# Gated cross-attention with a mixture-of-experts layer: expert rows turned by VectorE instead of TensorE

## The reference

```python
x = x + tanh(g_xattn[0]) * mlstm(layernorm(x), ctx, ctx, ...)    # x: 16 x 256 x 512, float32
x = x + tanh(g_ffn[0]) * moe(layernorm(x), ...)

def moe(h):                                    # h as 4096 rows x 512; E = 16, K = 2, I = 256
    scores = softmax(h @ router_w.T)
    topk_w, topk_idx = top_k(scores, 2);  topk_w /= sum(topk_w)
    gates = zeros((T, E)).at[rows, topk_idx].add(topk_w)
    g = einsum('th,ehi->tei', h, expert_gate)  # expert_gate, expert_up: 16 x 512 x 256
    u = einsum('th,ehi->tei', h, expert_up)
    y = einsum('tei,eih,te->th', silu(g) * u, expert_down, gates)     # expert_down: 16 x 256 x 512
    return y + silu(h @ shared_gate) * (h @ shared_up) @ shared_down
```

## Time and profile before

| | us |
|---|---|
| median of 3 runs | 1118.34 |
| lowest and highest of them | 1115.02, 1119.09 |
| the profiled execution | 1122.74 |
| its span, first to last instruction | 1121.1 |
| busy TensorE, share of the span | 90% |
| busy VectorE, ScalarE, GpSimd | 68%, 35%, 38% |

### The profile page before, as it was taken

How to read it: one execution, slowest core, us unless ns; L and a number is a source line. 1 busy time by engine, 2 the same in 40 slices (tenths; PEclk the granted TensorE clock), 3 DMA queues, 4 the chain that set the end, 5 groups by cost and what they waited for, 6 DMA issues and landing times.

```text
span 1121.1 us, 20851 instructions
## 1 busy us (share of the span) xinstructions
PE 1008.5 (90%) x6427; PEld 850.0 (76%) x6427; DVE 757.2 (68%) x1983; ACT 391.6 (35%) x870; POOL 421.5 (38%) x318
## 2 busy tenths in 40 slices
PE   3779999999999999989884799999999999999882
PEld 1568988898889977869773588888888888887661
DVE  2787889888898887888867444444444444445666
ACT  2644445534454344454321132223323233221100
POOL 5010221122202222022225355667566667105675
PEclk9889999999999987989786899999999999999896
DMA  7340220222112212021118735655555563926887
GB/s 256 130 192 1 77 76 11 76 76 77 39 39 77 76 65 87 20 95 39 76 42 315 267 105 183 207 168 170 198 180 170 167 210 114 337 104 216 266 296 253
DMA packets 60037, 155.62 MB, mean 139 GB/s; under 512 B 7296, under 2 KB 7296, under 8 KB 58016
## 3 DMA queue, kind: packets, MB, share of 16 engines
q0 software_dynamic: 18448, 69.22, 18.3%
q1 hardware_dynamic: 29008, 62.93, 16.3%
q10 hardware_dynamic: 12480, 22.16, 5.5%
HBM read 93.46 MB, written 60.82 MB: 138 GB/s over the span
## 4 chain that ended last, share of the span: by engine, by line
PE 74%; DVE 10%; issue 7%; DMA 4%; POOL 2%; SPq 1%; ACT 1%; POOLq 0%; DVEq 0%; ACTq 0%
PE bank L1285 19%; PE bank L1148 12%; PE bank L1303 10%; PE bank L1159 4%; PE bank L1011 4%; PE bank L1076 4%; PE bank L1347 3%; PE bank L1273 3%; PE bank L1097 2%; PE bank L1100 2%; PE bank L1098 2%; POOL w_ring L705 2%; PE bank L1123 2%; DMA routed_x<-xn 2%; PE bank L1294 2%
## 5 line engine op out<-in xcount | busy, mean ns | idle before, releaser
L1285 PE MATMUL bank<-w_ring,x2nT 128*128 x948 | 242.0, 404 | 1.8 <-DVE x2nT L1854 1.8
L1285 PEld LDWEIGHTS bank<-w_ring,x2nT 128*128 128x128 f32 x948 | 174.5, 191 | 38.0 <-issue 2.6
L1148 PE MATMUL bank<-x2nT,w_ring 128*128 128x256 f32 x1152 | 149.9, 287 | 0.0
L574 POOL DMA_INDIRECT routed_x<-x2n,slot_u x64 | 66.0, 1031 | 206.3 <-DVE slot_u L1618 191.7
L1148 PEld LDWEIGHTS bank<-x2nT,w_ring 128*128 128x128 f32 x1152 | 142.5, 193 | 0.3
L1836 DVE SCALAR_TENSOR_TENSOR ctxT<-ctxT,bank 128x256 f32<-128x256 f32 x79 | 33.3, 422 | 141.0 <-ACT ctxT L939 141.0
L1303 PE MATMUL bank<-w_ring,sh_actT 128*128 x474 | 123.7, 396 | 1.1 <-DVE sh_actT L1849 1.1
L659 POOL TENSOR_TENSOR w_ring<-area,one 128x3072 fp32r<-128x3072 f32 x14 | 74.3, 5304 | 115.5 <-PE bank L1303 115.5
L1303 PEld LDWEIGHTS bank<-w_ring,sh_actT 128*128 128x128 f32 x474 | 88.9, 188 | 22.5 <-issue 1.4
L939 ACT ACTIVATE ctxT<-bank 128x256 f32<-128x256 f32 x79 | 30.5, 386 | 192.5 <-PE bank L1285 192.5
L662 POOL TENSOR_TENSOR w_ring<-area,w_ring 128x3072 fp32r<-128x3072 f32 x14 | 95.7, 6836 | 2.5 <-POOL w_ring L659 2.5
(11 more groups left out here) (229 smaller groups left out, 2024.4 us busy)
## 6 DMA issues: line engine op xcount, KB each, us to landing
routed_y<-cs_in ACTq DMA_DIRECT2D x79, 256.0 KB, 2.2
x2n<-routed_x SPq DMA_DIRECT2D x75, 256.0 KB, 2.9
base_out<-in_x_dram SPq DMA_DIRECT2D x16, 512.0 KB, 5.0
cs_in<-in_ctx_dram SPq DMA_DIRECT2D x16, 512.0 KB, 4.0
area<-n_L_ffn_expert_gate_dram POOLq DMA_DIRECT2D x16, 512.0 KB, 4.6
area<-in_L_ffn_expert_up_dram POOLq DMA_DIRECT2D x16, 512.0 KB, 5.5
area<-n_L_ffn_expert_down_dram POOLq DMA_DIRECT2D x16, 512.0 KB, 7.5
out_dram<-base_out SPq DMA_DIRECT2D x32, 256.0 KB, 4.0
```

The lines of the kernel that those rows point to most:

```text
L574: pool.indirect_dma_start(out=routed_x, in_=x2n[:, b.par, j, :], in_offset=None, out_offset=bass.IndirectOffsetOnAxis(ap=slot_u[:, b.par, ...
L1148: last = mm(gu_bank(b.n, m)[:, at:at + S], w[:, w_part, c, m * P:(m + 1) * P], x2nT[:, x_part, c, :], start=(c + p == 0), stop=(c == DC - ...
L1285: last = mm(bank[2 + t.par][:, :], xtT[:, x_part, t.par, c * P:(c + 1) * P], w_gu[:, bass.ds(slot, 1), w_part, c, :].rearrange("p a i -> p ...
```

## The change

SyncE and ScalarE load the rows of a tile by four DMAs instead of one. DMA q brings feature columns 128q to 128q+127 of all 128 rows into partitions 32q to 32q+31; each partition gets four pieces of 128 numbers, one from each group of 32 rows. VectorE then turns the tile with one `transpose` instruction, which turns each block of 32 x 32 by itself, from `xt` into the PSUM bank. Row p of the result holds, for chunk c, feature 4p + c, where before it was feature 128c + p; the gate and up weights are loaded in the same order. The down weights keep theirs.

```diff
-        xt_in = [event(f"xt_in{k}", 16) for k in range(XRING)]
+        xt_in = [event(f"xt_in{k}", 16 * NQ) for k in range(XRING)]      # QP = 32, NQ = 4
...
+        def load_rows(eng, row, k):
+            for q in range(NQ):
+                own = slice(q * QP, (q + 1) * QP)
+                eng.dma_start(xt[own, k, :].rearrange("t (g n) -> t g n", g=P // QP),
+                              routed_x[bass.ds(row, P), q * P:(q + 1) * P].rearrange("(g t) n -> t g n", t=QP)
+                              ).then_inc(xt_in[k].sem, 16)
...                                            (SyncE; ScalarE alike)
-                sp.dma_start(xt[:, k, :], routed_x[bass.ds(row, P), :]).then_inc(xt_in[k].sem, 16)
+                load_rows(sp, row, k)
...                                            (GpSimd, load_expert)
-                    src = of[bass.ds(e, 1)].rearrange("a (c p) i -> (a p) c i", p=P)
+                    src = of[bass.ds(e, 1)].rearrange("a (p c) i -> (a p) c i", p=P)     # gate and up
...                                            (ScalarE)
             def copy_x(t):
                 act.wait_ge(xt_turned.sem, xt_turned.upto(t.n))
+                act.wait_ge(gu_made.sem, gu_made.upto(t.n - 2))
...                                            (TensorE)
-            def turn_rows(n, t, k):
-                pe.wait_ge(xt_in[k].sem, n)
-                pe.wait_ge(xt_lo_made.sem, xt_lo_made.upto(t.n - 2))
-                for c in range(DC):
-                    last = tr(bank[t.par][:, c * P:(c + 1) * P], xt[:, k, c * P:(c + 1) * P], ident[:, :])
-                last.then_inc(xt_turned.sem, 1)
...
-            def gate_up(t, e, slot):
-                pe.wait_ge(expert_in.sem, e + 1)
-                pe.wait_ge(xt_lo_made.sem, xt_lo_made.upto(t.n))
-                pe.wait_ge(act_made.sem, act_made.upto(t.n - 2))
-                for c in range(DC):
+            def gate_up(t, e, slot, of):
+                if of[0] == 0:
+                    pe.wait_ge(expert_in.sem, e + 1)
+                    pe.wait_ge(xt_lo_made.sem, xt_lo_made.upto(t.n))
+                    pe.wait_ge(act_made.sem, act_made.upto(t.n - 2))
+                for c in of:
...
-                if ahead2:
-                    turn_rows(lap * 16 + 16, t + 2, k)
+                    gate_up(t + 1, e, slot, range(0, 1))
                 turn_act(t)
                 if ahead1:
-                    gate_up(t + 1, e, slot)
+                    gate_up(t + 1, e, slot, range(1, DC))
                 down(t)
...                                            (VectorE)
+            def turn_rows(t, k, lap):
+                dve.wait_ge(xt_in[k].sem, xt_in[k].upto(lap))
+                dve.wait_ge(xt_lo_made.sem, xt_lo_made.upto(t.n - 2))
+                v.transpose(bank[t.par][:, :].rearrange("p (c g t) -> p g c t", c=DC, t=QP),
+                            xt[:, k, :].rearrange("p (g d c) -> p g c d", c=DC, d=QP)).then_inc(xt_turned.sem, 1)
...
                 copy_actT(t)
                 if ahead2:
                     rest_x(t + 2)
+                if ahead3:
+                    turn_rows(t + 3, (t.n + 3) % XRING, (t.n + 3) // XRING)
                 if ahead1:
                     silu(t + 1)

+            turn_rows(Item(0, 0), 0, 0)
+            turn_rows(Item(0, 1), 1, 0)
             rest_x(Item(0, 0))
+            turn_rows(Item(0, 2), 2, 0)
             rest_x(Item(0, 1))
```

More of the change, by code:

```diff
@@ L51 @@
 YRING = 4
+QP = 32
+NQ = P // QP
 LATE_LOADS = [9, 16]
@@ L554, in load_expert @@
                 dn = stage[k][:, DC * 2 * I:EW].rearrange("p (c d) -> p c d", c=IC)
-                sides = ((gu[:, :, 0:I], expert_gate, DC), (gu[:, :, I:2 * I], expert_up, DC), (dn, expert_down, IC))
-                for to, of, c in sides:
-                    src = of[bass.ds(e, 1)].rearrange("a (c p) i -> (a p) c i", p=P)
+                for to, of in ((gu[:, :, 0:I], expert_gate), (gu[:, :, I:2 * I], expert_up)):
+                    src = of[bass.ds(e, 1)].rearrange("a (p c) i -> (a p) c i", p=P)
                     pool.dma_start(to, src).then_inc(expert_dma[k].sem, 16)
+                src = expert_down[bass.ds(e, 1)].rearrange("a (c p) i -> (a p) c i", p=P)
+                pool.dma_start(dn, src).then_inc(expert_dma[k].sem, 16)
             def values(b):
@@ L929, in _ @@
                 row = act.value_load(row_tab[0:1, n:n + 1], min_val=0, max_val=DUMP)
-                act.dma_start(xt[:, n, :], routed_x[bass.ds(row, P), :]).then_inc(xt_in[n].sem, 16)
+                load_rows(act, row, n)
             def copy_x(t):
                 act.wait_ge(xt_turned.sem, xt_turned.upto(t.n))
+                act.wait_ge(gu_made.sem, gu_made.upto(t.n - 2))
                 s.copy(xtT[:, 0, t.par, :], bank[t.par][:, :]).then_inc(xtT_made.sem, 1)
@@ L1287, in gate_up @@
                                   start=(c + p == 0), stop=(c == DC - 1 and p == 2))
-                last.then_inc(gu_made.sem, 1)
+                if of[-1] == DC - 1:
+                    last.then_inc(gu_made.sem, 1)
             def turn_act(t):
@@ L1306, in down, with expert_step @@
                 last.then_inc(y_made.sem, 1)
-            def expert_step(t, k, lap, ahead2=True, ahead1=True):
+            def expert_step(t, ahead1=True):
                 if ahead1:
@@ L1321, in _ @@
             pe.wait_ge(tables_made.sem, tables_made.upto(0))
-            turn_rows(16, Item(0, 0), 0)
-            turn_rows(16, Item(0, 1), 1)
             e = expert_of(Item(0, 0))
[L1325 to L1332, removed]
+            gate_up(Item(0, 0), e, pe.snap(e % RING), range(DC))
+            for n in range(TILES):
+                expert_step(Item(0, n), ahead1=n + 1 < TILES)
             def late_gate_up(u, k):
@@ L1855, in rest_x, with expert_step @@
                                 ).then_inc(xt_lo_made.sem, 1)
-            def expert_step(t, ahead2=True, ahead1=True):
+            def expert_step(t, ahead3=True, ahead2=True, ahead1=True):
                 copy_actT(t)
@@ L1881, in _ @@
             assert steps[0] == TABLE_STEPS + SLOT_STEPS
[L1882 to L1885, removed]
+            for n in range(2, TILES):
+                expert_step(Item(0, n), ahead3=n + 3 < TILES, ahead2=n + 2 < TILES, ahead1=n + 1 < TILES)
             dve.wait_ge(base_made.sem, base_made.upto(SH[LAST]))
```

## The result

The kernel after the change takes 1091.72 us (median of 4 runs, 1089.05 to 1093.56), beside it the kernel before 1118.71 (4 runs, 1115.02 to 1120.71). The ratio is 0.976 (95%: 0.973 to 0.978). The forecast was 1089 in a range of 1081 to 1112, faster: both hold. The profiled executions have spans of 1121.1 and 1090.1 us.

The account below looks back on a forecast made before the run. The prediction took TensorE alone to bound the steps: 32.5 us gained (74 x 0.44) less 3.0 at the start, 29.5 us off the median of 1118.3, gave 1089 us, range 1081 to 1112.

Parts of the forecast that it names:

- TensorE alone is the limit, and its work counts in full: Steps 4 to 76: removing 0.44 us of row transposes from TensorE shortens each step from 4.84 to 4.40 us.
- Chunk 0 covers silu: Each step: 0.70 us of the next gate_up before turn_act brings it 0.77 us later than silu needs, so no wait.
- rival (d): Each step: the chunk in front doesn't cover silu, TensorE stands 0.4 us before turn_act, nothing gained, 1118 us; chance 0.05.
- T = 0.7 us: VectorE, each step: one 128 x 512 transpose, called T, takes 0.7 us, hidden up to 1.6 us.
- The loop, 2.9 + T: VectorE loop turn_act, copy_actT, rest_x, transpose T, silu: limits the step at 2.9 us plus T, beyond T of 1.6.
- Rival (b): Transpose above 1.94 us makes the loop through VectorE the limit; at 2.7 us, 58 us more, 1176 us; chance 0.09.
- The transpose does not wait for GpSimd: VectorE's transpose, having one SBUF input, is not held up while GpSimd splits expert weights.
- Rival (a): VectorE's transpose waits for GpSimd's splits in 14 experts, 126 us more, 1215 us in all; chance 0.06.
- The weights, 0.5 us left: GpSimd's split in short experts: 12.7 us against 13.2 before TensorE needs it; cost zero, bad end 1 us x 7.
- rival (c): Faster, but less: short experts wait 1 us each and the start costs 7; 11 us less, 1100 us; chance 0.20.
- The start, 3.0 us: First steps: more load issues and turn_rows(4) before silu(2) delay step 4; 2.4 us plus 0.6 for a low clock.
- The loads, "hidden": Tile loads in small pieces: 1.0 us of DMA time per tile, landing 9.0 us at most against 17.6 ahead; no cost.

Follow-up runs that it names:

- e1: Kernel after the change, but all four chunks of the next gate_up come behind turn_act, none in front: 1117.52 us, ratio 0.9996.
- e2: Kernel before the change, its TensorE transposes kept, with only chunk 0 of the next gate_up moved in front of turn_act: 1119.44 us, ratio 0.999.
- p1: Separate kernel timing single VectorE instructions on 128 x 512, alone and beside GpSimd: float32 transpose 0.75 us plain, 1.11 us with the change's pattern.
- p2: Separate kernel timing transposes by read and write pattern, and tile loads beside big loads: longest landings 12.7 us whole, 17.8 by columns, 18.4 in dealt pieces.
- e5: Kernel after the change with half a second VectorE transpose (128 x 256) into a bank nobody reads: 1095.31 us, ratio 0.977.
- e4: Kernel after the change with a second, equal VectorE transpose into a bank nobody reads: 1123.35 us, ratio 1.004.
- e6: Kernel after the change with turn_rows of tile 4 moved on VectorE behind silu(2) and the slot instructions: 1087.53 us, ratio 0.971.
- e8: Kernel after the change with VectorE's slot instructions moved to steps 76 and 77 and turn_rows(4) behind silu(2): 1086.42 us, ratio 0.971.
- e7: Kernel after the change with the last shared expert's weights loaded in eight DMAs, one after each of eight tiles: 1087.08 us, ratio 0.971.
- the repeat: The kernel after the change, unedited, measured a second time: 1088.89 us, ratio 0.972.
- e3: Kernel before the change with only the loads changed, each tile in four column blocks to all partitions: 1116.92 us, ratio 1.000.

## Why the prediction was right

**TensorE alone is the limit, and its work counts in full.** Right: 4.84 became 4.39 (4.40 forecast), by the sum 0.22 + 2.78 + 1.41.

**Chunk 0 covers silu.** Right, and shown from both sides: without it (e1) the gain of 27 us is gone (0.997 to 1.002), which was rival (d); without the rest (e2) it gives nothing.

**T = 0.7 us.** The term that was mis-sized: 1.11. I went by the nearest rows in size and left out that the source is read in steps of 16 bytes; p1 and p2 show the 0.36 us of it. The Trainium skill's figure for VectorE, which gave 1.24 as an estimate, was the nearer one, but by luck: it is a figure for bf16, and in bf16 a plain transpose took 0.74 here. The 0.36 cost nothing, since 1.6 us were free (e5 shows 1.7 still free), and the sum did not hang on it.

**The loop, 2.9 + T.** 2.78 + T (e4). Rival (b) has its place and form right, its threshold 0.1 us too low. Within the prediction 2.9 and "up to T = 1.6" don't agree, for 2.9 + 1.6 is 4.50; the 1.6 is what e4 bears out.

**The transpose does not wait for GpSimd.** Right: all 79 take 1.06 to 1.12 us, and p1 shows it with GpSimd running beside it. Rival (a) is out. That the lock exists is shown by the copy with one input that did stand, so "one input" was not the whole of my argument: the transpose was safe for being neither a two-input instruction nor one of the quick kind. The Trainium skill ("SBUF — State Buffer", section "SBUF: two separate sides") has this as the lock of a two-port mode; the copy, 0.45 us alone against 0.72 into PSUM, fits that.

**The weights, 0.5 us left.** Right: TensorE has no wait on an expert's weights after the first; that half of rival (c) did not come.

**The start, 3.0 us.** Between 3.5 (down of tile 3) and 3.8 (turn_act of tile 4). gate_up(0) came 5.1 later against 5.3 forecast, and the order tile 4, silu(2), slots, copy_actT(2) is as worked out. e6 shows that moving turn_rows(4) alone does not take the loss away; the slots alone were not moved in any run; e8, with both moved, has 5.9 us less than the kernel after, the clock's part among them.

**The loads, "hidden".** In DMA time right: queue 1 takes 0.87 us of the 16 engines for each tile (6055 packets, 19.9% from 850 to 900 us) against 1.0 forecast. In landing wrong, at one place: 3.2 us. I had divided the longest landing of the kernel before, 9.0 us, into the 17.6 asked ahead, as if it would stay, and had counted the 17.6 from the first of the four issues. Cut in four and beside 6 MB of big loads the landing became 17.3, with 14.4 left for the last piece. e7 shows that it takes the big loads all at once. So rival (c), faster but less, came true by a third of its price and for another reason.

In sum 32.5 - 3.0 = 29.5 was forecast; 33.7 - 3.8 - 3.2 = 26.7 follows from the step lists, 2.8 less, and without the stall the two would agree to 0.4 us. That the medians miss by the same 2.7 us (1091.72 for 1089) proves little: the repeat, with a like stall (5.16 and 6.76 us), has 1088.89, and the two medians differ by as much as the miss.

What stays open: e3 loads in quarters too, beside the same big loads, and had 13.8 us at most where the kernel after had 17.3 (17.8 in its repeat). The pace of the steps is not the reason, for e1 and e4 have nearly the pace of e3 (4.77 and 4.79 us) and the loads of the change, and they have the stall and long landings, 18.1 us in e4 and in e1

```profile
DMA to landing us min/median/max: 1.8/2.0/18.9
```

What still differs is how the pieces are dealt, each to 32 partitions, and which engine sets a buffer free. p2 can't decide it, because both of its forms waited for the end of the big loads. No run here does.

## What to carry to other kernels

Taking work off the bounding engine pays only as far as the next late chain is covered; find that chain first (here at the stage's end, where the work was already missing) and move independent work in front of the wait. When loads are cut into smaller pieces, read the longest landing in the stretch where other queues move megabytes, not the median, and count the time it has from the last piece's issue. An instruction put ahead of a critical one on its engine brings its own wait along: place it behind.

## What had not been expected of the hardware

- A VectorE instruction that reads one fp32 number in every 16 bytes takes 0.36 us longer for 128 x 512, transpose and copy alike (1.11 and 1.08 against 0.75 and 0.72). A write in blocks costs nothing.
- A transpose in bf16 takes what fp32 takes: 0.74 us for 128 x 512.
- A one-input fp32 copy from SBUF to SBUF (0.45 us alone) stands behind GpSimd, three in 6.74 us; a copy into PSUM and a transpose into PSUM do not (three in 2.15 and 3.40 us), and a transpose from SBUF to SBUF does not either (three in 3.36).
- A DMA issue by SyncE, 0.317 us as a rule, took 5.3 us once while GpSimd's queue moved the large loads, and 4.9 to 6.6 in the six other kernels with loads to 32 partitions and the five big loads at once (1.5 in e3, 2.0 in e7).
- At the stage's start TensorE's granted clock fell to 0.50 behind a wait of 4.8 us before the change and behind one of 2.4 us after it, where down(2) took 2.92 us instead of 1.56. In e8, with shorter waits, it stayed at 1.00.
